# A sorted copy with a region of its own for each expert, filled batch by batch inside attention

## What is computed

```
x = x + xattn(layernorm(x), ctx, ...)          # 16 heads of 64, context of 1024 rows
h = layernorm(x)
probs = softmax(h @ router_w)                  # 8 experts
top_k_prob, top_k_idx = top_k(probs, 2)        # each row goes to two experts
out = x + h + shared_expert(h) + sum over e of gates[e] * expert_e(h)
# expert: gelu(h @ w_up) @ w_down, 256 -> 1024 -> 256, gelu by erf
```

## Time and profile before

| what | value |
|---|---|
| time, median of 3 executions | 2255.81 us (2253.99 to 2255.84) |
| profiled execution, span | 2252.6 us |
| PE busy | 2166.5 us, 96% |
| DVE / ACT / POOL busy | 78% / 60% / 19% |
| DRAM read, written | 181.44 MB, 79.72 MB |

### The profile page before, as it was taken

How to read it: one execution, slowest core, us unless ns; L and a number is a source line. 1 busy time by engine, 2 the same in 40 slices (tenths; PEclk the granted TensorE clock), 3 DMA queues, 4 the chain that set the end, 5 groups by cost and what they waited for, 6 DMA issues and landing times. The chain is left out here.

```text
span 2252.6 us, 48833 instructions
## 1 busy us (share of the span) xinstructions
PE 2166.5 (96%) x18002; PEld 1591.0 (71%) x18002; DVE 1763.5 (78%) x2342; ACT 1354.5 (60%) x1942; POOL 419.1 (19%) x358
## 2 busy tenths in 40 slices
PE   6999999999999999999999999999639999999999
PEld 5666666666666666666666666648539999999998
DVE  7999899889889899998988988995303565556775
ACT  6675676666567567666656755654114556556775
POOL 2110120111011011011101110004740122223222
PEclk9999999999999999999999999999659999999999
DMA  7344335335334533523533442244542454546773
GB/s 263 91 130 148 89 111 179 89 98 168 107 96 130 154 83 116 177 86 103 171 96 101 147 140 67 59 136 137 195 160 85 136 135 122 140 126 168 224 225 99
DMA packets 154291, 297.77 MB, mean 132 GB/s; under 512 B 34688, under 2 KB 79616, under 8 KB 152064
## 3 DMA queue, kind: packets, MB, share of 16 engines
q1 hardware_dynamic: 136176, 264.60, 38.2%
q0 software_dynamic: 17664, 30.45, 5.8%
q10 hardware_dynamic: 288, 0.26, 0.0%
HBM read 181.44 MB, written 79.72 MB: 116 GB/s over the span
## 5 line engine op out<-in xcount | busy, mean ns | idle before, releaser
L1039 ACT ACTIVATE probs<-scores 128x1024 f32<-128x1024 f32 x512 | 503.6, 1025 | 325.6 <-PE scores L754 312.8
L1345 DVE TENSOR_TENSOR sums<-sums,probs 128x1024 f32<-128x1024 f32 x384 | 470.2, 1225 | 14.2 <-issue 1.7
L880 PE MATMUL sum_ps<-probs,v_nat 128*64 128x512 f32 x2056 | 476.6, 599 | 3.6 <-DVE probs L1244 3.6
L754 PE MATMUL scores<-q_split,k_split 64*128 64x512 f32 x3072 | 415.2, 394 | 1.8 <-ACT probs L1039 1.8
L1244 DVE TENSOR_SCALAR probs<-probs 128x2048 f32<-128x2048 f32 x256 | 314.2, 1227 | 107.8 <-ACT probs L1039 107.4
L1927 PE MATMUL sum_ps<-down,hid_split 128*128 128x256 f32 x2640 | 361.4, 285 | 35.2 <-issue 34.1
L1927 PEld LDWEIGHTS sum_ps<-down,hid_split 128*128 128x128 f32 x2640 | 346.8, 193 | 54.9 <-issue 41.6
L1901 PE MATMUL scores<-xT,up 128*128 128x512 f32 (+1 forms) x1680 | 354.4, 351 | 19.0 <-issue 18.2
L2065 DVE TENSOR_TENSOR hid_split<-hid,hid_split 128x512 fp32r<-128x512 f32 x204 | 141.3, 692 | 252.4 <-ACT hid_split L1991 187.4
L754 PEld LDWEIGHTS scores<-q_split,k_split 64*128 64x128 f32 x3072 | 283.7, 185 | 55.1 <-ACT probs L1039 5.9
L1990 ACT ACTIVATE hid<-scores 128x512 f32<-128x512 f32 x220 | 131.5, 598 | 315.9 <-PE scores L1901 231.8
(11 more groups left out here) (229 smaller groups left out, 2284.4 us busy)
## 6 DMA issues: line engine op xcount, KB each, us to landing
k_two<-k_two SPq DMA_DIRECT2D x252, 128.0 KB, 2.3
w_all<-wpack SPq DMA_DIRECT2D x60, 512.0 KB, 4.2
raw<-L_ffn_routed_up SPq DMA_DIRECT2D x27, 1024.0 KB
raw<-L_ffn_routed_down SPq DMA_DIRECT2D x27, 1024.0 KB
rden<-rden_rows SPq DMA_DIRECT2D x128, 128.0 KB, 2.9
ctx_parts<-stage SPq DMA_DIRECT2D x28, 512.0 KB, 4.0
ctx_all<-ctx_parts SPq DMA_DIRECT2D x14, 1024.0 KB, 6.5
sorted_rows<-zero POOLq DMA_DIRECT2D x64, 162.5 KB, 2.5
```

Of the source, the lines that this page charges most:

```text
L754: last = pe.matmul(scores[j % 2][:, head], k_split[i][own, a, j * P:(j + 1) * P], q_split[i][own, m], start=n == 0, stop=n == 2)
L880: last = pe.matmul(sum_ps[64 * head:64 * head + 64, p % 2], v_nat[p // 2 % 2][:, j, cols:cols + 64], probs[:, j % PROBS, head], start=j == ...
L1039: act.activation(probs[:, j % PROBS], scores[j % 2][:], ACT.Exp, scale=float(HD) ** -0.5).then_inc(s_exp, 1)
L1345: v.tensor_tensor(to, to, probs[:, j % PROBS], ALU.add).then_inc(s_add, 1)
```

## The change

Each expert gets a region of its own in `sorted_rows`: 17 units (4096 rows and one more unit), so the tensor has 137 units. The place of a row is then known from the rows before it, and no count over all batches is needed. So in pass b of attention the rows of batch b - 2 are placed and written:

- slot 0 and 1, DVE, at their ends: `first_choice` (5 instructions) and `second_choice` (7), both with a wait after most;
- slot 2, PE: four small matmuls that rank the rows (`rank_by_columns`) into `sum_ps`, ACT copies them (`r_rank`) and later takes an exponential (`r_less`); PE waits for that copy before it reuses `sum_ps` in slot 3;
- slot 3, POOL: `route_scatter`, 32 small instructions with 29 waits for the one before, and then eight indirect DMAs;
- slot 4, ACT: `normalize`, which overwrites `xn`, waits for those eight instead of for the store to `normed`.

Passes 0 and 1 place rows of no batch, and set the counts back. The zeroing of `sorted_rows` by POOL is gone from attention. The last two batches are still placed and scattered behind attention (16 indirect DMAs instead of 64, tables for 8 tiles instead of 32). At the end SP writes eight blocks of 256 zero rows, one behind the last row of each expert, before it loads the first sorted rows. `xn` is now laid out with 260 numbers to a row, so that it can be scattered as it stands.

```
+        self.REG = self.B * self.N // self.U + 1
+        self.SPARE = self.E * self.REG
...
-        sp.sem_inc(s_xnout, 16)
...
-            sp.wait_ge(s_normed, normed)
-            sp.dma_start(xn_d[to].rearrange("(p t) d -> p t d", p=P), xn).then_inc(s_xnout, 16)
+            if isinstance(to, int):
+                sp.wait_ge(s_normed, normed)
+                sp.dma_start(xn_d[to - (B - 2)].rearrange("(p t) d -> p t d", p=P), xn).then_inc(s_xnout, 16)
...
+        spare = xs[sh.SPARE * sh.U:].rearrange("(p t) d -> p t d", p=P)
+        pool.wait_ge(prep["const"], 1)
+        pool.dma_start(spare, keep["zero"][:].unsqueeze(1).broadcast_to((P, sh.U // P, DW))).then_inc(s_zero, 16)
...
+        def then(b, ins):
+
+            step[0] += 1
+            ins.then_inc(s_rstep, 1)
+            pool.wait_ge(s_rstep, b * ROUTE_STEPS + step[0])
+            pool.sem_inc(s_rpass, 1)
+
+        def over_experts(b, dst, src):
+
+            then(b, pool.tensor_tensor(r_half[:], src[:, :, 0:4], src[:, :, 4:8], ALU.add))
+            then(b, pool.tensor_tensor(r_half[:, :, 0:2], r_half[:, :, 0:2], r_half[:, :, 2:4], ALU.add))
+            then(b, pool.tensor_tensor(dst, r_half[:, :, 0], r_half[:, :, 1], ALU.add))
+
+        def route_scatter(b):
+            step[0] = 0
+            then(b, pool.tensor_scalar(r_tok, r_tok, float(N), None, ALU.add))
+            then(b, pool.tensor_scalar(r_valid, r_tok[:, 0:1], 1.0, None, ALU.is_ge))
+            pool.wait_ge(s_rexp, b + 2)
+            over_experts(b, r_tot, r_less[:, :, 0:E])
+            then(b, pool.tensor_tensor(r_gate[0], r_tot, r_neg_one, ALU.pow))
+            then(b, pool.tensor_tensor(r_gate[1], r_less[:, :, E], r_gate[0], ALU.mult))
+            pool.tensor_copy(xn_rows[:, :, D], r_tok)
+            pool.tensor_scalar(xn_rows[:, :, D + 1], r_best[0], float(E), None, ALU.add)
+            pool.tensor_copy(xn_rows[:, :, D + 2], r_gate[1])
+            then(b, pool.tensor_tensor(xn_rows[:, :, D + 3], r_gate[0], r_gate[1], ALU.subtract))
+
+            pool.wait_ge(s_rrank, b + 1)
+            for t in range(QT):
+                then(b, pool.tensor_tensor(r_pos[:, t], r_rank[:, 0, t], r_next[:], ALU.add))
+                then(b, pool.tensor_tensor(r_next[:], r_rank[:, 1, t], r_next[:], ALU.add))
+            then(b, pool.tensor_tensor(r_next[:], r_next[:], region[:], ALU.subtract))
+            then(b, pool.tensor_scalar(r_next[:], r_next[:], r_valid, None, ALU.mult))
+            then(b, pool.tensor_tensor(r_next[:], r_next[:], region[:], ALU.add))
+            for n in range(2):
+                then(b, pool.tensor_tensor(r_tmp[:], r_sel[n][:], r_pos[:], ALU.mult))
+                over_experts(b, r_posf, r_tmp)
+                then(b, pool.tensor_copy(r_idx[n], r_posf))
+            for t in range(QT):
+                for n in range(2):
+                    pool.indirect_dma_start(xs, bass.IndirectOffsetOnAxis(ap=r_idx[n][:, t:t + 1], axis=0),
+                                            xn_rows[:, t], None).then_inc(s_rscat, 16)
+            assert step[0] == ROUTE_STEPS, step[0]
...
-            if p < PARTS:
-                pool.dma_start(flat[b * PARTS + p], keep["zero"][:]).then_inc(s_zero, 16)
...
+            if p == 3:
+                route_scatter(b)
...
+        def rank_by_columns(to):
+
+            chosen = r_both[:].rearrange("p t e -> p (t e)")
+            for c in range(2):
+                for n, m in enumerate((tri[:, halves(c)], ones[:, 0:64])):
+                    last = pe.matmul(to[halves(c), QT * E * n:QT * E * (n + 1)], m, chosen, start=n == 0, stop=True, skip_group_check=True)
+            last.then_inc(s_rps, 1)
...
+                    if p == 3:
+                        pe.wait_ge(s_rrank, b + 1)
...
+            if p == 2:
+
+                pe.wait_ge(s_dencp, b * PAIRS + (p + 2))
+                pe.wait_ge(s_rboth, b + 1)
+                rank_by_columns(sum_ps[:, before_p % 2])
...
+            if p == 2:
+                act.wait_ge(s_rps, b + 1)
+                act.activation(r_rank[:].rearrange("p n t e -> p (n t e)"), sum_ps[:, before_p % 2, 0:2 * QT * E], ACT.Copy).then_inc(s_rrank, 1)
...
+                act.wait_ge(s_rmax, b + 1)
+                act.activation(r_less[:], r_less[:], ACT.Exp).then_inc(s_rexp, 1)
...
-                    act.wait_ge(s_xnout, 16 * b + 16)
+                    act.wait_ge(s_rscat, SCATTERED * b + SCATTERED)
...
+        def first_choice(b):
+
+            step[0] = 0
+            less = r_less[:, :, 0:E]
+            v.wait_ge(s_lgout, b + 1)
+            then(b, v.tensor_reduce(r_mx, lg, AX.X, ALU.max))
+            then(b, v.tensor_tensor(less, lg, over_e(r_mx), ALU.subtract))
+            then(b, v.scalar_tensor_tensor(r_tmp[:], less, 0.0, e_bc, ALU.is_ge, ALU.mult))
+            then(b, v.tensor_reduce(r_best[0], r_tmp[:], AX.X, ALU.min))
+            then(b, v.tensor_tensor(r_sel[0][:], over_e(r_best[0]), e_bc, ALU.is_equal))
+
+        def second_choice(b):
+
+            less = r_less[:, :, 0:E]
+            then(b, v.scalar_tensor_tensor(r_below[:], r_sel[0][:], -1e30, less, ALU.mult, ALU.add))
+            then(b, v.tensor_reduce(r_less[:, :, E], r_below[:], AX.X, ALU.max))
+            v.tensor_tensor(r_tmp[:], r_below[:], over_e(r_less[:, :, E]), ALU.is_equal).then_inc(s_rmax, 1)
+            v.wait_ge(s_rmax, b + 1)
+            then(b, v.tensor_tensor(r_tmp[:], r_tmp[:], e_bc, ALU.mult))
+            then(b, v.tensor_reduce(r_best[1], r_tmp[:], AX.X, ALU.min))
+            then(b, v.tensor_tensor(r_sel[1][:], over_e(r_best[1]), e_bc, ALU.is_equal))
+            v.tensor_tensor(r_both[:], r_sel[0][:], r_sel[1][:], ALU.add).then_inc(s_rboth, 1)
+            assert step[0] == CHOICE_STEPS, step[0]
...
+            if p == 0:
+                first_choice(b)
+            if p == 1:
+                second_choice(b)
...
+        for e in range(E):
+            at = sp.value_load(pad_at[0:1, e:e + 1], min_val=0, max_val=(SPARE - 1) * U)
+            sp.dma_start(xs[bass.ds(at, U)].rearrange("(p t) d -> p t d", p=P),
+                         keep["zero"][:].unsqueeze(1).broadcast_to((P, U // P, DW))).then_inc(s_pad, 16)
+        sp.wait_ge(s_pad, 16 * E)
...
-        for b in range(B):
-            i = b % STAGES
-            if b < STAGES:
-                pool.wait_ge(s_stage[i], 16)
-            else:
-                pool.wait_ge(s_again[i], 16)
-            pool.tensor_copy(stage[i][:, :, D:], meta[:, b * QT:(b + 1) * QT]).then_inc(s_meta, 1)
-            pool.wait_ge(s_meta, b + 1)
+        for i in range(2):
+            pool.wait_ge(s_stage[i], 16)
+            pool.tensor_copy(stage[i][:, :, D:], meta[:, i * QT:(i + 1) * QT]).then_inc(s_meta, 1)
+            pool.wait_ge(s_meta, i + 1)
             for t in range(QT):
                 for n in range(2):
-                    pool.indirect_dma_start(xs, bass.IndirectOffsetOnAxis(ap=idx[n][:, b * QT + t:b * QT + t + 1], axis=0),
+                    pool.indirect_dma_start(xs, bass.IndirectOffsetOnAxis(ap=idx[n][:, i * QT + t:i * QT + t + 1], axis=0),
                                             stage[i][:, t], None).then_inc(s_scat[i], 16)
-            if 1 <= b <= B - STAGES:
-                nxt = b - 1 + STAGES
-                pool.wait_ge(s_scat[b - 1], 16 * 2 * QT)
-                pool.dma_start(stage[b - 1][:, :, 0:D], xn_d[nxt].rearrange("(p t) d -> p t d", p=P)).then_inc(s_again[b - 1], 16)
-        for i in range(STAGES):
-            pool.wait_ge(s_scat[i], 16 * 2 * QT * (1 + (i < B - STAGES)))
+        for i in range(2):
+            pool.wait_ge(s_scat[i], 16 * 2 * QT)
+        pool.wait_ge(*att["scattered"])
...
+        v.wait_ge(*att["scattered"])
+        v.tensor_copy(base[:, 0:1], next_rows[:, 0:1])
+        then(v.tensor_tensor(base[:, 1:E], next_rows[:, 1:E], run[:, 0:E - 1, NT - 1], ALU.subtract))
...
+                then(v.tensor_tensor(count, count, next_rows, ALU.add))
+                v.tensor_copy(pad_at[:], count)
+                then(v.tensor_tensor(count, count, region, ALU.subtract))
+                steps_below(units, unit_steps, KU)
```

More of the change, by code:

```diff
@@ L471, in attention @@
     n_mv = [sb(f"n_mv{i}", [P, QT, 2]) for i in range(NORMS)]
-    n_var, n_rstd, n_shift = ([sb(f"n_{what}{i}", [P, QT]) for i in range(NORMS)] for what in ("var", "rstd", "shift"))
+    n_all = [sb(f"n_{what}", [P, NORMS, QT]) for what in ("var", "rstd", "shift")]
+    n_var, n_rstd, n_shift = ([t[:, i] for i in range(NORMS)] for t in n_all)
     rw = sb("rw", [P, KD, E])
     bo_bc = sb("bo_bc", [P, D])
+    tri, region = keep["tri"], keep["region"]
+    lg = logits[:, 0:QT]
+    r_pos, r_tmp, r_both = (sb(f"r_{n}", [P, QT, E]) for n in ("pos", "tmp", "both"))
+    r_below = r_both
+    r_less = sb("r_less", [P, QT, E + 1])
+    r_sel = [sb(f"r_sel{n}", [P, QT, E]) for n in range(2)]
+    r_rank = sb("r_rank", [P, 2, QT, E])
+    r_few = sb("r_few", [P, 10, QT])
+    r_mx, r_tot, r_posf, r_neg_one, r_tok = (r_few[:, i] for i in range(5))
```

(33 more changed lines are left out.)

108 lines of the change are left out of this document (60 added, 48 removed).

## The result

The changed kernel takes 2321.69 us (2320.72 to 2322.06, four runs) against 2254.9 us (2252.72 to 2255.84, four runs): ratio 1.0297, 95% interval 1.0283 to 1.0312. It is slower by 66.8 us, where 2224 and a range up to 2262 had been forecast.

The account below looks back on a forecast made before the run. PE bounds attention (185.3 of 186.0 us) and the expert layer; beside the scatters it loses 71.8. Sum: 2252.6 - 71.8 + 12 + 4 + 6 + 18 = 2220.8, with 3.2 around the span 2224 us; range 2190 to 2262.

Parts of the forecast that it names:

- The slow stretch: Shared tiles behind attention, PE slow beside 64 POOL scatters: 71.8 us lost there, won back, less 12 for 16 remaining scatters.
- Rival C: Slowness comes with each scatter wherever it stands, 1.1 us each, also in attention: 2302 us, chance 0.05.
- rival D: Shared tiles' slow stretch set off by something other than the scatter count: nothing gained, 28 lost, 2284 us; chance 0.06.
- PE's rank products: Four small matmuls in slot 2 of attention, 0.5 us a pass: +4 in eight passes, bounds 2 and 7.
- DVE's choices: Ends of slots 0 and 1: second choice makes PE wait, first counted as hidden; +6 in all, bounds 0 and 27.
- POOL's chain: `route_scatter` in slot 3, 0.40 us a step: 30.5 against slack 27.8, DVE waits 2.7 in slot 4; +18 us.
- The bound: Upper bound of POOL's term: steps of 1.03 us, the shortest power, add 18 us: 7 x 21 = 147.
- Scatters in attention: Eight scatters in a group each pass, 10 us of POOL's time, cost PE 0 by slowing.
- SP: Eight address loads with a DMA each ahead of the sorted rows: 15 us fits in 20; cost 0, bound 5.
- Rival B: DVE's slot 4 wait for POOL eats the gain, even at 7.1 us; chances 0.11 slower, 0.04 no change, 0.08 from 2240.
- a rule of the Trainium skill: GpSimd shares SBUF interfaces with VectorE and contends with some DVE instructions; weighed against POOL's term, trace showed little of it.

Follow-up runs that it names:

- spread version: Changed kernel with choices, ranks and Exp a slot earlier, POOL's chain in three pieces, 24 waited steps instead of 29: 2219.65 us, later 2222.9 us.
- session 2: Runs sent together on another chip: changed kernel again 2320.57 us, scatters moved behind `rstd(4)` 2342.4, kernel before with gaps between scatter groups 2211.72; kernel before 2253.85.
- session 1: Runs sent together on one chip: changed kernel without scatters 2252.54 us, without small steps 2215.82, without both 2212.79, chain spread over three slots 2219.65; kernel before 2182.71.
- sessions 1 and 4: Session 4, the later of the two: kernel before with its 64 scatters in pairs, one pair a step, 2203.15 us against 2255.36, ratio 0.9775.

## Why the prediction was wrong, point by point

- *The slow stretch.* Right in place, cause and size. Forecast -71.8 + 12; undisturbed shared tiles take 168.1 us to step 56, so the kernel before loses 72.2 there and the changed one 10.5. Rival C (each scatter slows, wherever it stands) fell with the spread version in session 2, rival D with the shared tiles. That this gain depends on the session was not foreseen; all runs shown were of the one kind.
- *PE's rank products.* +4 for eight passes; PE's busy time rose by 0.4 in a pass, 3 in all.
- *DVE's choices.* +6; slots 1 and 2 of the changed kernel are longer by 1.9 us a pass, 13 in the seven passes of the loop and nothing in the last, of which 3 are PE's. So 10. Under-sized, within its bounds. I had counted the choice of slot 0 as hidden, and behind it PE waits up to 1.6 us for L1418 in slot 1. DVE comes to that line 2.2 us later in a pass than before (44.2 instead of 42.0), and the five steps of the choice are only 1.2 of them. The other 1.1 are one multiplication of DVE that now meets a `low_stage` of POOL and takes 1.76 us, where it took 0.69:

```profile
685.28 2.23 POOL L740 TENSOR_TENSOR stage<-whole,stage 128x512 fp32r<-128x512 f32 x1 [16.81 <-ACT stage L1212]
686.29 1.76 DVE L1498 TENSOR_TENSOR o<-sums,rden 128x512 f32<-128x512 f32 x1
```

- *POOL's chain: the step that failed.* The place was right, the engine that waits, the order of the waits, the slack (27.8; 27.2). The size of one factor was not: "I take 0.40" for a step, "a value near the copy, because the power's arithmetic is not that of an addition". Steps came every 0.92 us, and so the chain was 43.9 instead of 30.5 us and DVE's wait 16.7 instead of 2.7. The copy of 0.21 us in the earlier trace rows was measured where DVE was idle more than half the time; the power of 1.03 us that I set aside in the earlier trace rows was nearer. The sign stood in the earlier trace rows too: the same power of four numbers took 2.23 us in slot 4, beside a busy DVE, and 1.03 outside attention, and I took the 1.2 us between them for the power alone and not for the 29 steps. The bound (1.03, 147 us) held: the term came to 7 x 15.9 = 111 (slots 4 and 5), against 18.
- *Scatters in attention.* 0 forecast alone, 0 a pass measured alone; behind steps that overrun, 10 us a pass.
- *SP.* 0, and 0: eight stores in 9.95 us, rows asked for at 1806.12, needed at 1818.32.
- *The chances.* Rival B had its break-even worked out rightly (a wait of 7.1 us) and got 0.23 in all, and above 2262 it had what was left over. With a rule of the Trainium skill and its own bound both pointing there, that was too little.

The rows of SP and PE for the point on SP:

```profile
1806.12 1.51 SPq L1857 DMA_DIRECT2D rows<-sorted_rows  x2
```

```profile
1818.32 1.03 PE L2082 MATMUL proj<-ident,rows 128*128 128x128 f32 x8
```

## What to carry to other kernels

Price a chain of small GpSimd instructions by a row taken beside VectorE's long additions and clips, at about 0.95 to 1.2 us a step here, not by one taken while it is idle; and compare the chain's sum with the slack of what stands behind it in the same queue. Work that overruns one slack may cost a quarter of that when it is laid into several, and exchanging the order inside one queue may only change who waits. When a stall goes with a long series of transfers, first try to space the series out; it took one line here. And time a kernel in more than one session before a gain of 3% is believed, when the cause of what is won isn't known.

## What the runs showed of the hardware

- A small instruction of POOL takes 0.20 us while DVE is idle or at its `BATCH_NORM_STATS2`, and mostly 0.96 to 1.1 us beside DVE's additions and clips of 1.22 us, and ends with them; within one pass both are seen. It goes the other way too: a DVE multiplication that began while a POOL subtraction ran took 1.76 us instead of 0.69, in every loop pass of the changed kernel. The issue of an indirect DMA on POOL is held in the same way at times: 2.15 us instead of 0.96.
- PE's slow stretch beside a series of scatters was there in all measurements but those of session 1 (2246 to 2257 us for the kernel before against 2182.7), and sessions 1 and 4 ran on the same chip. Where it is, it needs the series to be dense: eight scatters in a loop pass of attention do nothing, 16 in a row cost 9 to 10 us, 64 with up to 40 in a row 72, 64 in groups of eight that wait for their landing 23, of which 20 are the late end, 64 in pairs held to PE's steps 14 to 21, of which 8 to 9 are the late end, 16 at one a step nothing. What passes between POOL's scatters and PE's instructions no run shows: PE's waits name only "issue", and the DMA engines were busy for 0.38 to 0.77 of the time there.
